# One weighing product per head with the high and low probability columns as the stationary matrix, three probability slots instead of four, new orders

## The chip, the cores and the metric

The kernel runs on one core of a Trainium2 chip. The metric is the device time of one execution in microseconds (us). The time before is 701.28 us, the median of three runs (700.39 to 702.39).

## The reference

A block of three parts works on x of shape (16, 64, 256): 16 batches of 64 query rows.

1. Cross-attention: queries from the normalised x, keys and values from a context of 1601 rows a batch, 16 heads of 16 columns each, softmax over the 1601 keys, an output projection, and the sum with x.
2. Self-attention with rotary positions over the 64 rows of a batch, 16 heads, and again a sum.
3. A routed layer of 8 experts (one for each row, with a capacity of 128 rows an expert), and again a sum.

The change is in the last product of the first part:

```
scores = einsum('bhqd,bhkd->bhqk', q, k) / sqrt(16)
attn   = softmax(scores, axis=-1)
ctx    = einsum('bhqk,bhkd->bhqd', attn, v)
```

All of it is f32 in the reference. The kernel splits f32 numbers into a bf16 high part (the upper half of the f32 word) and a bf16 low part (the rest), and multiplies high by high, high by low and low by high.

## The kernel before, in words

**Batches.** For each of 16 batches, the 1601 context rows are projected to keys and values (letter K in the orders: `project`, lines 812 and 821, in 15 units of work), the keys are stacked by DMA for the products, all scores are taken once for their maxima alone (letter m: `max_scores`, line 844, maxima by DVE at line 1511), and then the batch goes through 13 chunks of 128 keys (the last has 65).

**A chunk.** Two score halves on PE (letter s: `score_half`, line 872), two exponentials on ACT (letter e: `exponentials`, line 1242) into a slot `prob` of 1024 f32 columns (16 heads of 64 queries), one subtraction on POOL (letter p: `low_prob`, line 637; ten of the last batch's on DVE, line 1481) that writes the low parts, packed, into `plow`, and two weighing halves on PE (letter w: `weigh`, line 896). There are `NPAR` = 4 slots of `prob` and `plow`: an exponential into a slot waits until the weighing four chunks back is done.

**Weighing.** The probabilities are the stationary matrix, the values the moving one. A pair of heads (`hp`) makes one product: 128 stationary columns are two heads of 64 queries, and the moving columns are 32 low value columns, 32 high ones and a column of ones for the softmax's sum. With the high columns of the probabilities (every second bf16 of the f32 slot) all 65 columns are multiplied; with the low columns the last 33. Of each result only the blocks in which the head of the queries is the head of the values are used.

**The end of a batch.** DVE takes the reciprocal of the sums (line 1532), multiplies (line 1535, `divided`, letter v), and adds the two value parts in two reductions (line 1548, `attended`, letter a). The next batch's first weighing waits for the multiplication (`out_read`), since the bank `ps_out` is used again.

**Orders.** Each engine works through a string of letters written out in the file (`PE_PROGRAM`, `ACT_PROGRAM`, `DVE_PROGRAM`, `POOL_PROGRAM`); one letter is one call of a function, and its waits are on semaphores. DMAs are issued by SP in a fixed order, some by ACT and POOL at the start.

**Start.** x's first tile is normalised (DVE lines 1399 to 1407, POOL lines 560 and 564), queries are projected, weights are split into high and low parts (`weight_parts`), POOL issues ten DMAs with biases and the second part's weights (lines 585 to 593), and later folds the rotation into biases and weights (`fold`, letter f).

**After the batches.** Self-attention and experts run over eight tiles of 128 rows; this begins while the last batch is still being weighed. A bias is added there by a matmul whose stationary matrix is `pick`, a selecting column repeated 128 times (line 923).

Of the kernel before, what the change touches and what calls it, by code (L numbers as in the profile page):

```python
# [18 lines left out]
P = 128  # L19
D = 256  # L20
KT = D // P
HEADS = 16
DH = D // HEADS
B = 16
SQ = 64
# [9 lines left out]
VW = 66  # L35
OW = 65
NPAR = 4
# [46 lines left out]
def act_frees(b, u):  # L84
# [26 lines left out]
    ("KKKKKKKKKKKKKmmKmmKmKmKmmKmKmKmmKmKmmmKKmmKmKmmKmKmmKKmmKmKmmsKmsmsKmsmsKmwsmswmwsKsmswmwwmKmsswmKwm"  # L111
     "wssmKsmswmwswmsmKsmsmwwsmswmwsmsKmwmsswmKmwwwswswwwswsKmmsswwmKsmswwKmssmKwwmssmwwmKmmsKmmswKmmssKwm"
     "swsmwwmswsKmsmwKmsKmsswmwmKmsswwKmwwwmKwsmKsKmswsmwwsmsKmmssKwmwsmswwmKswmwmwwssKmsmKmwswmmsKmsswwmm"
     "sKsmmswwwsKmKmsswmwmKswmmKmswKswwwmwKswKswwsmmKsmmsKmsmsKwmwwswwmsmKsKwsmKssmKswswmmKmmwwssmKswmmwKm"
     "swwswmswmwwssmKwswmmsKmmwKmKwwmwwswKsKssKsKssmwmKmwsmswwmsmKmwswwmwsmKswmsKmwssmwmKmsmKwsmsmwwwssmKm"
     "wmsswwKmssKmmKmsmwwKmmwwwwKwwsmKsKssKmswsmKmswswmmKmsKsmwwmsKKmmsKswsmmwwswsmwmsKmKmswmKswswmmwsKwms"
     "wwsmwKsmmKsmmsKmmwwwwKwswmwKsswKssmKmssmwKsmwwmssmwKswmmwswsmwKswwsmmKmmKssKmmwwsswwmwmKwmsKsmwwmssK"
     "msmKmmsKmwwmKwmswwKmwsKssKsmsmwKwmssmKswsKwmmswwwmswmKsmsKmsswwwmmswsKmwmKmKmsmKwwsmswwmKswswmmsKmss"
     "wmKmmsKmmwwKwwwsmwKsswKswsmKsmmsKsmwswwwmsmsKmKwmswmwwsmswwKmssmKmwswsmKswmwmKmmswKmsKmmsswwmwsmsKms"
     "mKmmwwwKwwswmwKsswKssmmKmwssmKswmswwmsKsmKswwmmsswwKwsmwsKwwmsmKwmssmKsmmKmwmsKwwsmsmwKwmmssKmKmmKmm"  # L120
     "wwwsKwmswKswsKwswKmmssKwssmwwwsmwswmsmKmswwsmKsmwKsmmKmKwmswmsmKmswmwsmsKwwmwmKmssmKmssmKwwmmwwssKww"
     "wmKswmKssKsmmwswsKmssmwwmwsswmKmssmKwmwwwsswmwKsKsmsmKsmKsmmKmmwwwKmsswmwwwKwsmsmKmssmKmsmKmmwwwKwww"
     "msKssKswwsKmsmsKmwsmKmwsmwsmwwwKsmmsKmwsmswwwmsmKsswmmKmswsmwKmswwmsmsKsmKsmmwKsmsKmKwwwmwwmwKmwswKs"
     "wsmwmsKsmsKssmKmwmwwsmwwsKswmmswsKmwsmswwmKswmsmwsKmmKmsswwmwsKmmswKmwmKsswmKswwswmKmwKmmKswmKssmmws"
     "wwsmsKmsmsKwmmwsswmwwmswKwsmKmsmKmswsmmKmssmwwmwsmwswmsmKmwswsmwmsKmsmwswmsZmwswwsAwswwwwssOswsAwsww"
     "ssOswswwswswsswwswssswwsHsswwsJHswwsTJAVOTSVwwwwwSPPwHwwWJVAP2PTOoWSA2HOoJPPhVTHlWVJS2AToOhSPPhlWPl2"
     "PHAocWOJAV2OHToJhSHhlTlVJcVPTPSWSPP2Wo2PPoxhWlxghcxglx2gcogFhFlFFFFcFFFFFF", 1),
# [94 lines left out]
def build(nc, x, ctxT, wqT, wkT, wvT, bqk, woT, wqkv, wout, brows, wg, weT, be, consts, ones2, out):  # L222
# [3 lines left out]
    with ctx:  # L226
# [22 lines left out]
        vstack = [sb(f"vstack{p}", [P, NCH, HP, VW], bf16) for p in range(2)]  # L249
# [10 lines left out]
        oparts = sb("oparts", [P, 2, 4, 64])  # L260
        orec = sb("orec", [P, 2, 4])
# [21 lines left out]
        wqkv_sb = sb("wqkv_sb", [P, KT, 3 * D])  # L283
# [4 lines left out]
        bias3 = sb("bias3", [SEL, 3 * D])  # L288
        brot3 = sb("brot3", [SEL, 2 * D])
        pick = sb("pick", [SEL, E, P], bf16)  # L290
# [8 lines left out]
        rooms = [flat3(kstack[0]).bitcast(f32), vstack[0][:, :, :, :].rearrange("p c h n -> p (c h n)").bitcast(f32)]  # L299
# [26 lines left out]
        late_rooms = [flat3(kstack[1]).bitcast(f32), vstack[1][:, :, :, :].rearrange("p c h n -> p (c h n)").bitcast(f32)]  # L326
# [19 lines left out]
        late_rooms += [prob[n][:, :] for n in range(3)]  # L346
# [60 lines left out]
        out_inverse, out_read, att_done = sem("out_inverse"), sem("out_read"), sem("att_done")  # L407

# [37 lines left out]
        def v0_stage(u):  # L446

            return prob[(u - KUNITS) // 2][:, (u - KUNITS) % 2 * 512:(u - KUNITS) % 2 * 512 + 512]
# [1407 lines left out]
```

## Time and profile before

| | busy us | share of the span |
|---|---|---|
| PE (matmul) | 671.0 | 96% |
| PE weight loads | 507.2 | 72% |
| DVE | 552.5 | 79% |
| POOL | 549.0 | 78% |
| ACT | 443.4 | 63% |

The profiled execution has a span of 699.7 us from its first instruction to its last; its own time outside the profiler is not listed, and the three timed runs have a median of 701.28 us. The granted clock of PE is full in all 40 slices of the page. A busy time is the union of an engine's instruction durations; a matmul's duration contains its way through the array, which overlaps the next matmul, so the spacing of matmuls has to be read from their start times.

### The profile page before, as it was taken

The numbers are of one execution on the slowest core, as the hardware profiler recorded it, in microseconds if no ns is written. First come the engines' busy times: TensorE is split into PE (matmuls) and PEld (weight loads), VectorE is DVE, ScalarE is ACT, GpSimd is POOL, SyncE is SP. The second block draws the span as 40 slices with busy tenths as digits, with TensorE's granted clock in tenths as the row PEclk, the third lists the DMA queues.
The fourth block names the chain that finished last, engine by engine and source line by source line (L and its number), as shares of the span: only waits on it lengthen the run. The fifth ranks groups of instructions, "written<-read, shape, count | busy, mean of one in ns | idle before, by whom it ended". The sixth has DMA issues, their size and how long they took to land.

```text
span 699.7 us, 21737 instructions
## 1 busy us (share of the span) xinstructions
PE 671.0 (96%) x8632; PEld 507.2 (72%) x8681; DVE 552.5 (79%) x1138; ACT 443.4 (63%) x885; POOL 549.0 (78%) x374
## 2 busy tenths in 40 slices
PE   4799999999999999999999999999999998899897
PEld 2556786877777877787778777877777786677673
DVE  4697877868888878778787868787868788888867
ACT  2446766666666666676767666767675787665830
POOL 7759999999699889798989789889788786723422
PEclk9999999999999999999999999999999999999999
DMA  8587055454445454545353645363543450000212
GB/s 309 143 213 214 27 138 162 99 155 97 150 113 155 105 164 92 160 107 165 93 165 84 178 102 159 85 187 89 169 97 104 100 164 4 2 2 9 91 69 91
DMA packets 45610, 84.20 MB, mean 120 GB/s; under 512 B 8668, under 2 KB 28420, under 8 KB 45508
## 3 DMA queue, kind: packets, MB, share of 16 engines
q1 hardware_dynamic: 43896, 80.13, 41.9%
q0 software_dynamic: 912, 2.14, 1.0%
q8 instruction: 70, 1.15, 0.7%
q10 hardware_dynamic: 704, 0.55, 0.3%
q14 instruction: 28, 0.23, 0.1%
HBM read 36.89 MB, written 6.55 MB: 62 GB/s over the span
## 4 chain that ended last, share of the span: by engine, by line
PE 82%; DVE 5%; DMA 5%; SPq 2%; issue 2%; POOL 2%; ACT 2%; ACTq 0%; DVEq 0%; POOLq 0%
PE ps_kv L821 17%; PE ps_kv L812 16%; PE ps_score L872 12%; PE ps_out L896 12%; PE ps_front L844 12%; PE ps_score L920 2%; SPq L502 2%; DMA kstack<-khigh 2%; PE ps_out L912 1%; DMA cbuf<-in_ctxT 1%; PE ps_kv L783 1%; DMA wq_sb<-in_wqT 1%; PE ps_front L920 1%; PE ps_front L853 1%; PE ps_kv L920 1%
## 5 line engine op out<-in xcount | busy, mean ns | idle before, releaser
L637 POOL TENSOR_TENSOR plow<-prob 128x1024 bf16<-128x1024 f32 (+1 forms) x198 | 372.1, 1898 | 58.8 <-ACT prob L1242 56.3
L1511 DVE TENSOR_REDUCE maxes<-ps_front 128x1 f32<-128x512 f32 (+1 forms) x416 | 267.1, 666 | 57.2 <-PE ps_front L844 53.9
L1242 ACT ACTIVATE prob<-ps_score 128x512 f32<-128x512 f32 (+1 forms) x416 | 236.2, 598 | 71.0 <-PE ps_score L872 61.9
L872 PE MATMUL ps_score<-qstack,kstack 98*128 98x128 bf16 (+1 forms) x1664 | 150.5, 219 | 0.8 <-ACT prob L1242 0.5
L844 PE MATMUL ps_front<-kstack,qstack 96*128 96x512 bf16 (+1 forms) x512 | 145.4, 333 | 2.7 <-DMA kstack<-khigh 1.9
L872 PEld LDWEIGHTS ps_score<-qstack,kstack 98*128 98x128 bf16 (+1 forms) x1664 | 112.1, 98 | 33.7 <-ACT prob L1242 1.9
L896 PE MATMUL ps_out<-vstack,prob 128*128 128x65 bf16 (+1 forms) x1664 | 113.6, 194 | 0.7 <-POOL plow L637 0.3
L821 PE MATMUL ps_kv<-w_hi,cbuf 128*128 128x256 bf16 (+1 forms) x402 | 109.7, 273 | 0.9 <-DVE vstack L1501 0.9
L1494 DVE SCALAR_TENSOR_TENSOR klow<-ps_kv,bcol,khigh 128x512 bf16<-128x512 f32 (+1 forms) x123 | 76.8, 629 | 42.5 <-ACT khigh L1220 42.0
L821 PE MATMUL ps_kv<-w_hi,clow 128*128 128x256 bf16 (+1 forms) x402 | 109.5, 272 | 0.0
L821 PE MATMUL ps_kv<-w_lo,cbuf 128*128 128x256 bf16 (+1 forms) x402 | 109.5, 272 | 0.0
L1220 ACT ACTIVATE khigh<-ps_kv,bcol 128x512 bf16<-128x512 f32 (+1 forms) x123 | 72.7, 593 | 56.0 <-PE ps_kv L812 54.6
L578 POOL TENSOR_TENSOR clow<-cbuf 128x801 bf16<-128x801 f32 (+1 forms) x63 | 96.5, 1542 | 12.8 <-DMA cbuf<-in_ctxT 12.8
L896 PE MATMUL ps_out<-vstack,plow 128*128 128x33 bf16 (+1 forms) x1664 | 102.4, 178 | 0.0
L896 PEld LDWEIGHTS ps_out<-vstack,prob 128*128 128x128 bf16 (+1 forms) x1664 | 91.0, 98 | 15.4 <-POOL plow L637 1.2
L1228 ACT CAST vstack<-ps_kv 128x512 bf16<-128x512 f32 (+1 forms) x105 | 58.2, 554 | 51.7 <-PE ps_kv L821 51.6
L812 PE MATMUL ps_kv<-clow,w_hi 128*128 128x512 bf16 (+1 forms) x245 | 78.0, 331 | 2.4
L812 PE MATMUL ps_kv<-cbuf,w_lo 128*128 128x512 bf16 (+1 forms) x242 | 78.7, 338 | 0.1
L896 PEld LDWEIGHTS ps_out<-vstack,plow 128*128 128x128 bf16 (+1 forms) x1664 | 74.7, 96 | 0.0
L1501 DVE TENSOR_TENSOR vstack<-ps_kv,vstack 128x512 bf16<-128x512 f32 (+1 forms) x105 | 67.7, 645 | 5.5 <-ACT vstack L1228 5.0
L812 PE MATMUL ps_kv<-cbuf,w_hi 128*128 128x512 bf16 (+1 forms) x211 | 66.9, 332 | 0.3 <-DVE klow L1494 0.2
L844 PEld LDWEIGHTS ps_front<-kstack,qstack 96*128 96x128 bf16 x512 | 42.2, 97 | 12.3 <-issue 2.8
(290 smaller groups left out, 858.7 us busy)
## 6 DMA issues: line engine op xcount, KB each, us to landing
kstack<-khigh SPq DMA_DIRECT2D x256, 100.1 KB, 2.2
cbuf<-in_ctxT SPq DMA_DIRECT2D x15, 1601.0 KB, 7.2
kstack<-klow SPq DMA_DIRECT2D x128, 100.1 KB, 2.2
qstack<-q_blocks SPq DMA_DIRECT2D x48, 64.0 KB, 2.3
q_blocks<-qbd SPq DMA_DIRECT2D x16, 128.0 KB, 2.0
cbuf<-in_weT SPq DMA_DIRECT2D x2, 1024.0 KB, 7.8
slot_x<-att_all SPq DMA_DIRECT2D x8, 128.0 KB, 7.1
vstack<-slot_x SPq DMA_DIRECT2D x4, 256.0 KB, 3.6
```

Of the source, the lines that this page charges most:

```text
L578: nc.gpsimd.tensor_tensor(clow[par][:, k, a:a + n], cbuf[par][:, k, a:a + n], c_high(par, k, a, n), ALU.subtract).then_inc(clow_done, 1)
L637: nc.gpsimd.tensor_tensor(plow[slot][0:n, :], prob[slot][0:n, :], p_high(slot, 0, HP * P)[0:n], ALU.subtract).then_inc(plow_gps, 1)
L812: mm = nc.tensor.matmul(ps[:, 0:nn], w[0][:, k, t * P:(t + 1) * P], rhs, start=(j == 0), stop=(j == len(terms) - 1))
L821: mm = nc.tensor.matmul(ps[0:nn, a * D:(a + 1) * D], lhs, w[1][:, k, :], start=(j == 0), stop=(j == len(terms) - 1))
L844: mm = nc.tensor.matmul(ps[:, at:at + nn], qstack[par][0:96, q_at(hp), :], kstack[par][0:96, hp, n0:n0 + nn], start=True, stop=True)
L872: mm = nc.tensor.matmul(ps_score[0:nn, h % NSB, j * P:(j + 1) * P], kstack[par][0:98, hp, n0:n0 + nn], qstack[par][0:98, q_at(hp), :], sta ...
L896: mm = nc.tensor.matmul(o[:, 32 * part:OW], lhs, vstack[par][0:nn, k, hp, 32 * part:OW], start=(k == 0 and part == 0 and hp % 4 == 0), sto ...
L1220: nc.scalar.activation(khigh[:, t, n0:n0 + nn], kv_bank(b, u)[:, 0:nn], ACT.Identity, bias=bcol[:, 1, t:t + 1]).then_inc(high_done, 1)
L1242: nc.scalar.activation(prob[slot][0:nn, e * 512:e * 512 + 512], ps_score[0:nn, h % NSB, :], ACT.Exp)\
L1494: nc.vector.scalar_tensor_tensor(klow[:, t, n0:n0 + nn], kv_bank(b, u)[:, 0:nn], bcol[:, 1, t:t + 1], khigh[:, t, n0:n0 + nn], ALU.add, AL ...
L1501: nc.vector.tensor_tensor(v[:, :, :, 0:32], kv_bank(b, u)[0:rows, 0:nch * D].rearrange("p (c h d) -> p c h d", c=nch, h=HP), v[:, :, :, 32 ...
L1511: nc.vector.reduce_max(maxes[:, hp:hp + len(unit), n], ps[:, 0:len(unit) * nn].rearrange("p (h k) -> p h k", k=nn), AX.X).then_inc(m_free, 1)
```

## The change

The slot of a chunk becomes one f32 array of 16 heads, two parts and 64 columns. The exponential writes part 0 in f32. The subtraction reads part 0 and its upper bf16 halves, and writes the low part as bf16 into the upper halves of part 1. So the 128 upper halves of one head (64 high, 64 low columns) are one stationary matrix with a step of two bf16. The moving matrix is that head's 16 low value columns, 16 high ones and a column of ones: 33 columns. Rows 0 to 63 of the result belong to the high, rows 64 to 127 to the low probabilities; the product of low by low is now included. There are three slots, of 2048 f32 columns each, in the memory of the four slots and their `plow` before.

At the end of a batch ACT copies rows 64 to 127 of the result (letter D, `low_outputs`), DVE adds them to rows 0 to 63, and then takes reciprocal, multiplication and one reduction over 64 rows, where it had 128 rows and two reductions.

To make room, the rotation weights and biases are loaded into parts of `att_all` that are not yet used (`wqk_raw`, `bias_raw`), the load of the former is issued in `fold` 0 instead of at the start, and `pick` is one column, repeated by the operand's access pattern. All four orders are written anew.

```diff
-VW = 66
-OW = 65
-NPAR = 4
+VW = 33
+OW = 33
+NPAR = 3
...
-        prob = [sb(f"prob{p}", [P, HP * P]) for p in range(NPAR)]
-        plow = [sb(f"plow{p}", [P, HP * P], bf16) for p in range(NPAR)]
+        prob = [sb(f"prob{p}", [P, HEADS, 2, SQ]) for p in range(NPAR)]
+        prob_flat = [a[:, :, :, :].rearrange("p h r q -> p (h r q)") for a in prob]
...
+        def p_parts(slot, part):
+            return prob_flat[slot].bitcast(bf16)[:, 1::2].rearrange("p (h r q) -> p h r q", h=HEADS, r=2)[:, :, part, :]
+        def p_columns(slot, h):
+            return prob_flat[slot].bitcast(bf16)[:, 4 * SQ * h + 1:4 * SQ * (h + 1):2]
...
-                nc.gpsimd.tensor_tensor(plow[slot][0:n, :], prob[slot][0:n, :], p_high(slot, 0, HP * P)[0:n],
+                nc.gpsimd.tensor_tensor(p_parts(slot, 1)[0:n], prob[slot][0:n, :, 0, :], p_parts(slot, 0)[0:n],
                                         ALU.subtract).then_inc(plow_gps, 1)
...
-                for part in range(2):
-                    for hp in range(4 * half, 4 * half + 4):
-                        o = ps_out[:, half, (hp % 4) * OW:(hp % 4 + 1) * OW]
-                        lhs = plow[slot][0:nn, hp * P:(hp + 1) * P] if part else p_high(slot, hp * P, P)[0:nn]
-                        mm = nc.tensor.matmul(o[:, 32 * part:OW], lhs, vstack[par][0:nn, k, hp, 32 * part:OW],
...
+                for h in range(HP):
+                    mm = nc.tensor.matmul(ps_out[:, half, h * OW:(h + 1) * OW], p_columns(slot, HP * half + h)[0:nn],
+                                          vstack[par][0:nn, k, HP * half + h, :],
...
+            def low_outputs(b):
+                act.wait_ge(pv_done, NCH * (b + 1))
+                wait(act, out_read, b)
+                wait(act, att_done, b)
+                nc.scalar.copy(oparts[:, :, :, :], ps_out[SQ:2 * SQ, :, 0:HP * OW].rearrange("p a (h c) -> p a h c", c=OW))\
+                    .then_inc(out_low, 1)
...
             def divided(b):
-                dve.wait_ge(pv_done, NCH * (b + 1))
...
+                dve.wait_ge(out_low, b + 1)
+                rows = ps_out[0:SQ, :, 0:HP * OW].rearrange("p a (h c) -> p a h c", c=OW)
+                nc.vector.tensor_tensor(rows, rows, oparts[:, :, :, :], ALU.add).then_inc(out_sums, 1)
+                dve.wait_ge(out_sums, b + 1)
+                nc.vector.reciprocal(orec[:, :, :], rows[:, :, :, 2 * DH]).then_inc(out_inverse, 1)
                 dve.wait_ge(out_inverse, b + 1)
...
+                nc.vector.tensor_tensor(oscaled, rows[:, :, :, 0:2 * DH],
+                                        orec[:, :, :].unsqueeze(3).to_broadcast([SQ, 2, HP, 2 * DH]), ALU.mult)                    .then_inc(out_read, 1)
...
 DVE_PROGRAM = [
-    ("jKKKkKBzKkzKKCKmmmmm...
+    ("jBKkKzKCkKKKKzkKmzmm...
```

## Rows read from the trace of the kernel before

**Rows 1.** The page: the span, then busy time, share and instructions of each engine

```profile
span 699.7 us, 21737 instructions
...
PE 671.0 (96%) x8632; PEld 507.2 (72%) x8681; DVE 552.5 (79%) x1138; ACT 443.4 (63%) x885; POOL 549.0 (78%) x374
```

**Rows 2.** Busy time by stretch: us, busy of each engine, PE clock, DMA

```profile
60.00:580.00 520.00, 516.04 (x7155) 398.20 (x7191) 415.30 (x796) 351.51 (x664) 456.37 (x266) 1.00 0.48 128
580.00:700.00 120.00, 109.33 (x1172) 79.76 (x1178) 95.86 (x254) 66.81 (x177) 48.69 (x59) 1.00 0.12 39
```

**Rows 3.** PE's waits from 60 to 580 us: us in total, times, longest

```profile
PE ps_out L896 <- POOL plow L637: 0.3, 1, 0.3
PE ps_out L896 <- DVE oparts L1535: 0.3, 1, 0.3
```

**Rows 4.** PE's timeline near 304.5 us: start, us, engine, line, operands, count

```profile
304.41 0.39 PE L872 MATMUL ps_score<-qstack,kstack 98*128 98x128 bf16 x4
304.64 0.29 PE L896 MATMUL ps_out<-vstack,prob 128*128 128x65 bf16 x4
304.77 0.25 PE L896 MATMUL ps_out<-vstack,plow 128*128 128x33 bf16 x4
304.87 0.38 PE L872 MATMUL ps_score<-qstack,kstack 98*128 98x128 bf16 x4
```

**Rows 5.** The page's groups of line 896: count, busy us, mean ns, idle before

```profile
L896 PE MATMUL ps_out<-vstack,prob 128*128 128x65 bf16 (+1 forms) x1664 | 113.6, 194 | 0.7 <-POOL plow L637 0.3
...
L896 PE MATMUL ps_out<-vstack,plow 128*128 128x33 bf16 (+1 forms) x1664 | 102.4, 178 | 0.0
L896 PEld LDWEIGHTS ps_out<-vstack,prob 128*128 128x128 bf16 (+1 forms) x1664 | 91.0, 98 | 15.4 <-POOL plow L637 1.2
...
L896 PEld LDWEIGHTS ps_out<-vstack,plow 128*128 128x128 bf16 (+1 forms) x1664 | 74.7, 96 | 0.0
```

**Rows 6.** PE's timeline at the start, six 65-column matmuls, first and last

```profile
16.43 0.19 PE L812 MATMUL ps_kv<-cbuf,w_hi 128*128 128x65 bf16 x1
...
16.59 0.19 PE L812 MATMUL ps_kv<-cbuf,w_lo 128*128 128x65 bf16 x1
```

**Rows 7.** POOL's groups by form: count, busy us, mean ns, idle before

```profile
L637 POOL TENSOR_TENSOR plow<-prob 128x1024 bf16<-128x1024 f32 x183 | 343.8, 1898 | 42.6 <-ACT prob L1242 40.1 <-PE ps_kv L812 0.8 <-PE ps_out L896 0.5
...
L648 POOL TENSOR_TENSOR vstack<-prob,vstack 128x512 bf16<-128x512 f32 x6 | 6.7, 1128 | 3.0 <-ACT vstack L1194 2.9
...
L616 POOL TENSOR_TENSOR brot<-brot 8x512 f32<-8x512 f32 x3 | 3.1, 1032 | 0.2
```

**Rows 8.** DVE's groups by form

```profile
L1548 DVE TENSOR_REDUCE att_all<-oparts 64x128 f32<-64x256 f32 x32 | 13.3, 417 | 0.7
L1535 DVE TENSOR_TENSOR oparts<-ps_out,orec 128x512 f32<-128x512 f32 x16 | 11.1, 692 | 0.6
```

**Rows 9.** ACT's groups by form

```profile
L1242 ACT ACTIVATE prob<-ps_score 128x512 f32<-128x512 f32 x384 | 218.3, 598 | 67.2 <-PE ps_score L872 59.1 <-PE ps_out L896 4.8
...
L1228 ACT CAST vstack<-ps_kv 128x512 bf16<-128x512 f32 x90 | 52.7, 585 | 50.1 <-PE ps_kv L821 50.1
```

**Rows 10.** The timeline from batch 14's last weighing to batch 15's first

```profile
575.74 0.25 PE L896 MATMUL ps_out<-vstack,plow 65*128 65x33 bf16 x4
...
576.79 0.19 DVE L1532 RECIPROCAL orec<-ps_out 128x8 f32<-128x8 f32 x1
577.02 0.69 DVE L1535 TENSOR_TENSOR oparts<-ps_out,orec 128x512 f32<-128x512 f32 x1
...
577.86 0.29 PE L896 MATMUL ps_out<-vstack,prob 128*128 128x65 bf16 x4 [0.26 <-DVE oparts L1535]
```

**Rows 11.** The timeline of the start: POOL's last issue, DVE's variance, POOL's root, PE

```profile
18.26 0.81 POOL L593 DMA_DIRECT2D wg_sb<-in_wg  x1
...
19.77 0.15 DVE L1407 TENSOR_SCALAR ve<-mv 128x1 f32<-128x1 f32 x1
...
20.01 0.58 POOL L560 TENSOR_TENSOR rs<-ve,half_neg 128x1 f32<-128x1 f32 x1 [0.94 <-DVE ve L1407]
...
21.98 0.33 PE L773 MATMUL ps_kv<-cst,h 128*128 128x128 f32 x1 [2.06 <-POOL h L564]
```

More of the change, by code:

```diff
@@ L248, in build @@
         kstack = [sb(f"kstack{p}", [P, HP, SKP], bf16) for p in range(2)]
-        vstack = [sb(f"vstack{p}", [P, NCH, HP, VW], bf16) for p in range(2)]
+        vflat = [sb(f"vstack{p}", [P, NCH * HEADS * VW], bf16) for p in range(2)]
+        vstack = [a[:, :].rearrange("p (c h n) -> p c h n", c=NCH, h=HEADS) for a in vflat]
         qstack = [sb(f"qstack{p}", [P, HP, P], bf16) for p in range(2)]
-        prob = [sb(f"prob{p}", [P, HP * P]) for p in range(NPAR)]
-        plow = [sb(f"plow{p}", [P, HP * P], bf16) for p in range(NPAR)]
+        prob = [sb(f"prob{p}", [P, HEADS, 2, SQ]) for p in range(NPAR)]
+        prob_flat = [a[:, :, :, :].rearrange("p h r q -> p (h r q)") for a in prob]
         maxes = sb("maxes", [P, HP, NPIECE])
@@ L287, in build @@
         wg_sb = sb("wg_sb", [P, KT, E])
[L288 removed]
+        bias3 = sb("bias3", [SEL, D])
         brot3 = sb("brot3", [SEL, 2 * D])
[L290 removed]
+        pick = sb("pick", [SEL, E], bf16)
         picked = sb("picked", [SEL, 2, E])
@@ L345, in build @@
         pT = [a.rearrange("p (h n) -> p h n", h=HP) for a in kbd_flat]
-        late_rooms += [prob[n][:, :] for n in range(3)]
+        late_rooms += [prob_flat[n][:, 0:HP * P] for n in range(3)]
         late_used += [0, 0, 0]
@@ L922, in product3 @@
                 for i, (cols, row, bias) in enumerate(biases):
-                    mm = nc.tensor.matmul(dst[:, cols], pick[:, row, :], high(bias), start=False,
+                    mm = nc.tensor.matmul(dst[:, cols], pick[:, row:row + 1].to_broadcast([SEL, P]), high(bias), start=False,
                                           stop=(i == len(biases) - 1), skip_group_check=True)
@@ L1081, in experts @@
                          lambda k: we_low[k][:, cols],
-                         [(slice(a * D, (a + 1) * D), 2 * pair + a, bias3[:, 2 * D:3 * D]) for a in range(2)])\
+                         [(slice(a * D, (a + 1) * D), 2 * pair + a, bias3[:, :]) for a in range(2)])\
                     .then_inc(ev["e_ps"], 1)
@@ L1347, in _ @@
                     copy_shift(*next(shifts))
+                if letter == "D":
+                    low_outputs(next(outputs))
                 if letter == "Z":
@@ L1543, in attended @@
                     dve.wait_ge(zeros_sent, 16 * (E + BY_SLOT))
[L1544 to L1548 removed]
+                dst = att_all[SQ * (b % 2):SQ * (b % 2) + SQ, b // 2 * D:b // 2 * D + D]
+                nc.vector.reduce_sum(dst.rearrange("p (h d) -> p h d", h=HEADS),
+                                     oscaled.rearrange("p a h (r d) -> p (a h) d r", r=2), AX.X).then_inc(att_done, 1)
             def constants():
```

175 lines of the change are left out of this document (85 added, 90 removed).

## The prediction

> **What bounds the kernel now.** I read four things in turn. First the busy shares: TensorE (PE) is busy 96% of a span of 699.7 us, no other engine over 79% [rows 1]. Busy time of pipelined matmuls can overstate, so second the stretches: between 60 and 580 us, where the batches run, PE is busy 516.0 of 520 us and GpSimd (POOL) 456.4 [rows 2]. Third PE's waits in that stretch: the two that touch this change come to 0.3 us each, once in 520 us [rows 3]. So PE's instruction stream is the clock of that stretch, and whatever shortens the stream shortens the kernel, until another engine runs out: POOL has 64 us to spare there (520 - 456). The last 120 us differ: PE is busy 109.3 of 120 [rows 2]; there, chains across engines decide.
>
> Fourth the spacing of the weighing matmuls, since the mean durations contain the pipeline's drain. A weighing half is four 65-column matmuls with the high columns, then four 33-column ones with the low columns. The first four take 0.13 us from start to start of the next group (32.5 ns each), the second four 0.10 us (25 ns each) [rows 4]. There are 1664 of either kind [rows 5], in 416 such pairs of groups.
>
> The profile's span is 699.7 us against a median of 701.28: 1.6 us lie around the span. I sum against the span and add 1.6.
>
> **The weighing.** A half becomes eight matmuls, one per head, each with 128 stationary and 33 moving columns. The number of matmuls and weight loads stays 3328. The 1664 wide ones become narrow: 1664 x (32.5 - 25) ns = 12.5 us less on PE, if a narrow matmul keeps its 25 ns. Halving the columns doesn't halve the time: 33 columns cost 25 ns, not half of 32.5.
>
> What is new is that every stationary operand is now read with a step of two bf16; before, the low half was packed. Its load might be the limit at 33 columns. Bounds: at most 32.5 ns, since the high group keeps that with stepped loads [rows 4]; its 32.5 come from the 65 columns, for 65-column matmuls whose stationary is packed also start 0.16 us / 5 = 32 ns apart [rows 6]. At least 25 ns, the shortest that the trace shows for 33 columns. A stepped load lasts 98 ns, a packed one 96 [rows 5]: next to no difference. I take 25 ns. Ends of the range: -12.5 us at 25; at 32.5 the high half gains nothing and the low half loses as much, +12.5 us.
>
> The Trainium skill speaks against the term: "TensorE: Matmul & The Clock Gate", section "Back-to-back issue gap", gives about 81 ns per matmul for a sustained stream of load and matmul pairs at 128 columns. If loads set such a floor, fewer columns would save nothing and the weighing would give 0. The trace disagrees: four 128-column score matmuls, each with its own load, take 0.23 us, 57 ns each [rows 4], so the measurement decides.
>
> **The subtraction for the low part** (POOL, ten on VectorE, DVE) now writes every second bf16 in runs of 64 instead of a packed row. No row shows that. POOL's packed form takes 1898 ns; a 512-element POOL operation with f32 output (elements 4 bytes apart) takes 1032 ns, one with operands broken into runs of 32 takes 1128 [rows 7], 9% more. So bounds 1.89 to 2.07 us; I take 1.90, since the step in bytes is that of an f32 row. Cover: POOL's 64 us. At 2.07 its load in the stretch rises by some 185 x 0.17 = 31 us to 488, of about 508 left. It hides, though thinly: in the first windows POOL is fuller than on average. The exponentials' writes in runs of 64 and V's in runs of 16: V's cast, already in runs of 32, takes 585 ns for 512 elements against 598 for the unbroken exponential [rows 9]; 0, bounds +-5%, hidden by both engines' idle time.
>
> **The end of a batch.** Before: reciprocal, then multiplication, 0.20 + 0.69 us on DVE [rows 10]. After: ACT copies the low 64 rows (528 elements; about 0.60, by the exponential [rows 9]), DVE adds (528/512 x 0.69 = 0.71 [rows 8]), reciprocal, multiplication. That is 1.3 us more work and two more hand-offs, estimated at 0.2 each from the 0.15 between the multiplication's end and the next weighing [rows 10]: 1.7 us more, some 3.0 us from a batch's last weighing to the next one's first. The reductions fall from two of 0.417 [rows 8] to one of 512 elements, about 0.7. DVE gains 0.6 us a batch, ACT 0.6, both off the bound. Queued behind the wait on DVE are maxima (which free the front banks) and K's low parts; behind ACT's copy, exponentials.
>
> What covers it is PE's other work between these weighings. Counting letters of the new PE order with the spacings of the trace, that is 3.3 to 7.4 us at 13 of the 15 boundaries, 1.1 us at the first and 0.2 at the last. The first loses 3.0 - 1.1 = 1.9 us. The last lacks 2.8, but is followed by a batch that ACT, DVE and POOL pace anyway, and DVE is already waited for there [rows 10]; I take +1.5 of 0 to 2.8. If the cover fails everywhere (other work ahead in the two queues), it is up to 15 x 1.7 = 26 us.
>
> **Three slots for four.** Between a chunk's last scores and its first weighing lies the exponential (0.6), the subtraction (1.9) and hand-offs (0.4): 2.9 us. In the new order PE has a median of 4.8 us of other work there (5.8 before); in batches 0 to 13 just two chunks have less, by 1.9 us together, and they stand at the first boundary, already counted. So 0 here; bounds 0 to +6, since exponentials must now wait for a weighing three chunks back instead of four.
>
> **Startup.** PE waits 2.06 us for the second query tile's normalised rows, whose chain starts with DVE's variance at 19.77; POOL starts the root at 20.01 after issuing DMAs until 19.07 [rows 11]. The new DVE order takes that variance after two low parts instead of four, so POOL starts right after its issues: 1.0 us less. The weights' split moves ahead into DVE's idle time. The rotation weights' load goes from POOL's queue at the start to the bias fold; its reader is several steps later. Bounds -2 to +1. The 38 bias matmuls with a broadcast column: 0.
>
> **Sum:** -12.5 - 1.0 + 1.9 + 1.5 = -10.1; 699.7 - 10.1 + 1.6 = 691.2. Forecast **691 us**.
>
> **Rivals.**
> *Longer path and fewer slots eat the gain.* Both lengthen PE's dependence on three other engines; the order was written out for assumed durations, and PE waits where one is late. For it: the median cover fell from 5.8 to 4.8 us, and the path grew at every boundary. Against: PE waited 0.3 us on this path in 14 batches. With 0.6 us lost per boundary and some 2 us to slots, 9 + 2 = 11 us: 702.
>
> *Stepped loads set the pace* (the other side). At 33 columns the load no longer hides behind the matmul, on all 3328. It decides from about 28 ns: from there the gain, 1664 x (32.5 - x) - 1664 x (x - 25), falls under the 2.4 us of the other terms. At 32.5: 691 + 25 = 716; at 30, 691 + 17 = 708. Against: 98 to 96 ns.
>
> *POOL becomes the bound.* It decides where 456 + 185 x d exceeds 516, d = 0.32 us, a subtraction of 2.2 us. At 2.4: 456 + 93 = 549, 33 us over the old stretch, 735; against it, the largest growth in a like row is 9%. At 2.07 only the full early windows suffer, some 4 us: 695.
>
> *It saves nothing*, for 25 ns may hold only in groups of four: 699 to 704.
>
> **How the numbers follow.** Forecast 0.66 (685 to 698), path and slots 0.15 (698 to 705), stepped loads 0.08, POOL 0.08, nothing saved 0.03. What this kernel's measurement tells from no change is about 0.3%, 2.1 us. Faster by more: all of the forecast, 0.05 of path and slots, 0.04 of the small ends of loads and POOL: 0.75. Same: 0.07 of path and slots, 0.03 of the others: 0.10. Slower: 0.15. Range 685 to 704; above it lies most of the loads and POOL cases (0.13), below it 0.06 for a startup and tail better than counted.
>
> **What would show it.** In the profile after: eight 33-column matmuls in 0.20 us (0.26 for the stepped-load case); POOL's subtraction at 1.9 us (over 2.2 is the POOL case), with POOL's waits for exponentials shrinking from the idle time it has; PE busy at 99% in the batches, its waits on the attention rows once at the first boundary and once at the last (at most boundaries: the path case); the wait for the second query tile at about 1 us. A loss of PE time in the last 120 us of over 4 us would also make the prediction wrong: there the orders differ most, and I counted only one boundary.

## The result, and the profile after

The changed kernel takes 724.24 us (median of six runs, 722.85 to 729.34), the kernel before beside it 701.92 (700.39 to 702.57): 1.0331 times as long, with an interval of 1.0302 to 1.0361. I forecast 691 us and a range that ended at 704: sign and size are wrong.

The page of the changed kernel first: PE is busy 12 us longer, in a span 27 us longer [rows 1].

```profile
span 726.6 us, 21820 instructions
...
PE 683.2 (94%) x8681; PEld 506.5 (70%) x8681; DVE 561.5 (77%) x1138; ACT 458.6 (63%) x901; POOL 550.1 (76%) x376
```

What the sum spoke of came about, as far as single instructions go. PE's timeline: eight weighing matmuls of 33 columns take 0.20 us (302.71 to 302.91), 25 ns each, as taken from [rows 4].

```profile
302.71 0.36 PE L906 MATMUL ps_out<-vstack,prob 128*128 128x33 bf16 x8
302.91 0.38 PE L885 MATMUL ps_score<-qstack,kstack 98*128 98x128 bf16 x4
```

The groups of the page say the same of the two operations that no row of before showed: the subtraction takes 1898 ns and the stepped load 97 ns [rows 5, 7].

```profile
L650 POOL TENSOR_TENSOR prob<-prob 128x1024 bf16<-128x1024 f32 (+1 forms) x198 | 372.3, 1898 | 65.6 <-ACT prob L1252 63.8
...
L906 PEld LDWEIGHTS ps_out<-vstack,prob 128*128 128x128 bf16 (+1 forms) x3328 | 121.7, 97 | 22.6 <-issue 2.2
```

The stretches show where the time went (columns as in [rows 2]). From 60 to 580 us PE is busy 513.2 of 520. The last 147 us end 27 us later than before; PE is idle 23 of them, where it was idle 11 of 120, and its mean granted clock is 0.93, in one stretch 0.83. Before, it was 1.00 throughout.

```profile
60.00:580.00 520.00, 513.20 (x7117) 389.03 (x7116) 416.65 (x792) 362.10 (x671) 456.97 (x266) 0.99 0.48 128
...
580.00:727.00 147.00, 123.91 (x1263) 89.08 (x1260) 103.78 (x259) 72.13 (x187) 48.67 (x60) 0.93 0.10 32
...
660.00:680.00 20.00, 14.96 (x162) 10.92 (x163) 13.42 (x34) 12.09 (x34) 7.39 (x8) 0.83 0.08 28
```

PE's waits from 580 us on have two long ones that the kernel before lacks. The longest of the kernel before there is 1.3 us, on DVE's `klow`.

```profile
PE ps_out L916 <- DVE prob L1604: 4.0, 2, 3.8
PE ps_out L1071 <- DVE mask L1676: 3.0, 1, 3.0
```

I divide each kernel at the start of its last group of weighing matmuls, and call the time from there to the start of PE's last group of matmuls the tail (self-attention and experts). These are the two groups in the kernel before, and then in the one after: the tail grew from 91 to 113 us.

```profile
604.87 0.25 PE L896 MATMUL ps_out<-vstack,plow 65*128 65x33 bf16 x4
...
696.17 0.39 PE L923 MATMUL ps_front<-bias,pick 72*128 72x256 bf16 x2
```

```profile
610.29 0.37 PE L906 MATMUL ps_out<-vstack,prob 65*128 65x33 bf16 x8
...
723.06 0.39 PE L933 MATMUL ps_front<-bias,pick 72*128 72x256 bf16 x2
```

### The profile page after: what moved, and what is told of

It is laid out like the page before. It is cut to its first block, busy times and chain, and to the rows that moved or that the text cites. A ratio compares the mean times of both kernels' runs of the same rounds, so it can differ in the third digit from the quotient of the medians.

```text
span 726.6 us, 21820 instructions
## 1 busy us (share of the span) xinstructions
PE 683.2 (94%) x8681; PEld 506.5 (70%) x8681; DVE 561.5 (77%) x1138; ACT 458.6 (63%) x901; POOL 550.1 (76%) x376
## 4 chain that ended last, share of the span: by engine, by line
PE 81%; DMA 5%; DVE 3%; SPq 3%; issue 3%; ACT 3%; POOL 2%; ACTq 0%; POOLq 0%; DVEq 0%
PE ps_kv L834 17%; PE ps_kv L825 14%; PE ps_score L885 12%; PE ps_front L857 12%; PE ps_out L906 10%; DMA kstack<-khigh 3%; SPq L512 2%; PE ps_score L930 2%; PE ps_front L930 2%; PE ps_kv L930 2%; PE ps_out L922 2%; POOL prob L650 1%; PE ps_kv L796 1%; SPq L505 1%; DMA wq_sb<-in_wqT 1%
## 5 line engine op out<-in xcount | busy, mean ns | idle before, releaser
L650 POOL TENSOR_TENSOR prob<-prob 128x1024 bf16<-128x1024 f32 (+1 forms) x198 | 372.3, 1898 | 65.6 <-ACT prob L1252 63.8
L1252 ACT ACTIVATE prob<-ps_score 128x512 f32<-128x512 f32 (+1 forms) x416 | 236.2, 597 | 70.6 <-PE ps_score L885 43.4
L885 PE MATMUL ps_score<-qstack,kstack 98*128 98x128 bf16 (+1 forms) x1664 | 155.8, 221 | 2.2 <-ACT prob L1252 2.0
L857 PE MATMUL ps_front<-kstack,qstack 96*128 96x512 bf16 (+1 forms) x512 | 147.5, 336 | 7.4 <-DMA kstack<-khigh 6.5
L906 PEld LDWEIGHTS ps_out<-vstack,prob 128*128 128x128 bf16 (+1 forms) x3328 | 121.7, 97 | 22.6 <-issue 2.2
L885 PEld LDWEIGHTS ps_score<-qstack,kstack 98*128 98x128 bf16 (+1 forms) x1664 | 113.4, 99 | 32.8 <-ACT prob L1252 4.4
L906 PE MATMUL ps_out<-vstack,prob 128*128 128x33 bf16 (+1 forms) x3328 | 132.9, 178 | 2.6 <-DVE prob L1501 1.4
L1238 ACT CAST vstack<-ps_kv 128x512 bf16<-128x512 f32 (+1 forms) x105 | 60.8, 580 | 49.8 <-PE ps_kv L834 49.4
L825 PE MATMUL ps_kv<-cbuf,w_hi 128*128 128x512 bf16 (+1 forms) x246 | 80.6, 341 | 1.3 <-DVE klow L1514 1.2
L825 PE MATMUL ps_kv<-cbuf,w_lo 128*128 128x512 bf16 (+1 forms) x246 | 80.8, 341 | 0.0
L834 PEld LDWEIGHTS ps_kv<-w_lo,cbuf 128*128 128x128 bf16 (+1 forms) x402 | 39.9, 99 | 8.1 <-issue 0.5
L834 PEld LDWEIGHTS ps_kv<-w_hi,cbuf 128*128 128x128 bf16 (+1 forms) x402 | 39.8, 99 | 6.0 <-issue 1.0
```

Source lines behind the costliest of these rows:

```text
L650: nc.gpsimd.tensor_tensor(p_parts(slot, 1)[0:n], prob[slot][0:n, :, 0, :], p_parts(slot, 0)[0:n], ALU.subtract).then_inc(plow_gps, 1)
L825: mm = nc.tensor.matmul(ps[:, 0:nn], w[0][:, k, t * P:(t + 1) * P], rhs, start=(j == 0), stop=(j == len(terms) - 1))
L834: mm = nc.tensor.matmul(ps[0:nn, a * D:(a + 1) * D], lhs, w[1][:, k, :], start=(j == 0), stop=(j == len(terms) - 1))
L857: mm = nc.tensor.matmul(ps[:, at:at + nn], qstack[par][0:96, q_at(hp), :], kstack[par][0:96, hp, n0:n0 + nn], start=True, stop=True)
L885: mm = nc.tensor.matmul(ps_score[0:nn, h % NSB, j * P:(j + 1) * P], kstack[par][0:98, hp, n0:n0 + nn], qstack[par][0:98, q_at(hp), :], sta ...
L906: mm = nc.tensor.matmul(ps_out[:, half, h * OW:(h + 1) * OW], p_columns(slot, HP * half + h)[0:nn], vstack[par][0:nn, k, HP * half + h, :] ...
```

## The experiments

Each experiment gives its edit and what follows; the times stand in one table behind them. "Old" orders are those of the kernel before. Differences are against runs of the kernel before on the same chip.

**The narrow product alone (e1).** Old kernel and orders; all 3328 weighing matmuls have 33 columns. Left out: the high columns with the low value columns.

```diff
-mm = nc.tensor.matmul(o[:, 32 * part:OW], lhs, vstack[par][0:nn, k, hp, 32 * part:OW],
+cols = slice(32 - 32 * part, OW - 32 * part)
+mm = nc.tensor.matmul(o[:, cols], lhs, vstack[par][0:nn, k, hp, cols],
```

> The kernel before with one edit: the matmul on the high part moves 33 columns in place of 65, as the matmul on the low part does (the high part's product with the low values is left out). Each weighing then has the changed kernel's price, 8 matmuls of 25 ns, and orders, four slots and the out path stay as before. Theory T (the loss sits in the new orders): 689 to 694 us at a granted clock of 1.0. Rival N (a narrow moving side leaves TensorE too little work and its clock falls): 710 to 725 us with the clock below 0.99. Rival P (TensorE's saved time was not on the path): 699 to 703 us. Rival S (three slots and the longer out path): as T, since neither is in this kernel.

Measured: -8.2 us. Narrow columns help, by two thirds of the 12.5 that I counted. The tail is as before.

**The old product with the new orders (e2), and with the new tail alone (e3).** e2 takes all new order strings, e3 the new ones only from the letter Z on (the last batches' end and the tail; four letters w that the new tail lacks stand ahead of Z).

```diff
 # e3, PE_PROGRAM, around Z
-...ZmwswwsAwswwwwssOswsAwsw...
+...wwwwZmwswsAswswAswswswwssOws...
```

> The kernel before with the changed kernel's four written orders (ScalarE's without its 16 new letters D); old product, four slots. Theory T: 718 to 736 us and a granted clock below 0.99, since the orders alone bring the waits. Rivals N and S: 699 to 704 us at a clock of 1.0, since the product, the slots and the out path are the old ones.

> The kernel before with its own orders up to the letter Z (the last batch) and the changed kernel's orders from there on. Theory T, if the tail's order holds most of the loss: 715 to 725 us, with the 90 us behind the last weighing grown by 15 to 21 us. If T holds but the loss sits in the batches' order: 699 to 704 us. Rivals N and S: 699 to 704 us.

Measured: +27.2 and +20.4. The new orders slow down a kernel that has none of the new product, and most of it is the tail's order. e3's waits are those of the kernel after, to the digit:

```profile
PE ps_out L906 <- DVE prob L1585: 4.0, 2, 3.8
...
PE ps_out L1061 <- DVE mask L1657: 3.0, 1, 3.0
```

**Narrow product and new orders (e4), and that with three slots (e8).** e4 is e1 with the new orders; e8 lets it use three of its four slots.

```diff
 # e8
+SLOTS_USED = 3
-slot = i % NPAR
+slot = i % SLOTS_USED
...
-wait(act, pv_done, i - NPAR + 1)
+wait(act, pv_done, i - SLOTS_USED + 1)
```

> Both edits: the kernel before with 33 columns in every weighing matmul and with the changed kernel's orders (without D); four slots and the old out path stay. Theory T: 712 to 726 us, near the changed kernel's 724, with the clock below 0.99. Rival N: 710 to 726 us also. Rival S (slots and out path): 686 to 696 us, since both are the old ones. Read with the run of narrow matmuls alone and the run of the orders alone it tells whether the two add up.

> The old product with 33 columns and the new orders (721.5 us), with three of its four probability slots used. If the third slot's loss is what still parts it from the changed kernel (724.2 us): 723 to 726 us, with more exponentials waiting for a slot and keys' waits of 5 us or more. If the longer out path is: 720 to 722.5 us.

Measured: +19.9 and +18.2. Product and orders add up (27.2 - 8.2 = 19.0). The third slot costs nothing that can be seen: the two intervals overlap.

**The tail's two waits.** In e5 two of e3's POOL letters I (the conversion of expert weights) change place, one to a later and one to an earlier point; in e6 PE multiplies idle matrices (56 and 44 matmuls of 128 columns) during e3's two long waits.

```diff
 # e5, POOL_PROGRAM, its end
-...RrssRtItstssRYRIRYgYgggg
+...RrssRttstIIssRYRRYgYgggg
 # e6
+if t == 4: pe.wait_ge(ev["x2"], t + 1); keep_busy(0, 56)
+if g == 2: pe.wait_ge(ev["lg"], b); keep_busy(1, 44)
```

> The old product with the new tail (722 us), with two letters of GpSimd's order moved: the third and fourth conversion of expert weights (1.88 us each) run behind the scatter's reads, away from the two VectorE instructions that took 2.66 us (usually 0.41) and 1.76 us (usually 0.16) beside them. If those collisions make TensorE's two long waits of the tail (3.78 and 3.01 us): the waits shrink by some 1.9 and 1.6 us, less clock is lost behind them, 714 to 719 us. Rival (the waits come from TensorE's order, which leaves no other work there): the waits move to what is late next, 720 to 723 us.

> The old product with the new tail (722 us), with idle matmuls (56 and 44 of 128 columns, results unused) put on TensorE into its two long waits of the tail, so that it works while it waits. If the low clock behind these waits costs real time: the stretches at half clock behind them vanish, and with them the 4 us of TensorE time lost in them, 716 to 720 us. If the tail is bound by the chain between the engines and not by TensorE's speed: 721 to 724 us, the clock at 1.0 all the same.

Measured: +14.1 and +14.3, against e3's +20.4; the tail shrinks by some 4 us in either. e6's interval lies clear of e3's; e5's runs spread from 715.1 to 723.1 us and its interval overlaps e3's, so for e5 the reading rests on the trace: the shorter tail, and two waits that are halved.

```profile
PE ps_out L906 <- DVE prob L1585: 2.1, 2, 1.9
...
PE ps_out L1061 <- DVE mask L1657: 1.4, 1, 1.4
```

In e6 the clock stays full where e3's falls; the stretches of e3, then of e6:

```profile
650.00:670.00 20.00, 14.81 (x138) 9.48 (x131) 13.13 (x36) 10.21 (x30) 9.16 (x10) 0.83 0.06 20
675.00:695.00 20.00, 15.57 (x136) 12.56 (x135) 11.24 (x37) 7.57 (x20) 4.79 (x6) 0.91 0.20 64
```

```profile
650.00:670.00 20.00, 17.93 (x213) 13.37 (x212) 14.83 (x41) 11.97 (x36) 9.48 (x11) 1.00 0.06 21
675.00:695.00 20.00, 18.43 (x192) 14.89 (x193) 11.91 (x41) 7.08 (x20) 4.79 (x6) 1.00 0.22 77
```

So both causes work in the tail, the waits and the clock behind them. In either run some 16 of the tail's 20 us remain, but not all of that is of another origin: e6 takes away the clock's part and leaves the two waits in place, and e5 leaves about half of them.

**The changed kernel with the old tail (e7), with four slots (g3), with both (g4).** e7's old tail has some letters behind Z shifted, as three slots want it; g3 is the change with `NPAR = 4`; g4 is g3 with the old tail, without four letters w that the new batch orders have ahead of Z.

```diff
 # g3, g4
-NPAR = 3
+NPAR = 4
```

> The changed kernel with the tail's orders of the kernel before (from the letter Z on, six letters shifted so that three slots suffice); product, slots, out path and the batches' orders are the changed kernel's. Theory T (the tail's order holds most of the loss): 702 to 709 us, that is 724 less 15 to 22. Rivals: if the new product itself needs the longer tail, 718 to 726 us.

> The changed kernel with four slots in place of three, nothing else. If the third slot costs: 715 to 721 us. If it costs nothing, as in the old product under these orders: 722 to 726 us.

> The changed kernel with four slots and the tail's orders of the kernel before from the letter Z on (no letters shifted in TensorE's order; ScalarE's two letters D added). Theory T: the changed kernel's last weighing (610.7 us) and the old tail behind it (91 us), 702 to 707 us, so 17 to 22 us off the changed kernel. If the old tail does not fit the new batches: 710 us or more.

Measured: +9.3, +22.6 and +1.2. Four slots change nothing by themselves (724.56 us, the change 724.24). g3 and g4 differ in the tail's order alone, and by 21 us. The stretch from the last weighing to the end of PE's work, g3 and then g4:

```profile
607.27:719.21 111.94, 97.35 (x861) 68.43 (x860) 78.47 (x225) 50.18 (x137) 35.46 (x43) 0.94 0.12 37
```

```profile
607.06:698.61 91.55, 88.29 (x847) 63.09 (x847) 72.56 (x219) 48.43 (x134) 30.28 (x37) 1.00 0.15 49
```

Both begin it at 607 us. Of the 20.4 us between them PE is idle 11.3 more (14.6 against 3.3) and busy 9.1 more; at a clock of 0.94 some 13 us run at half speed, which can account for up to 6.7 of the 9.1, and 14 more matmuls stand behind the last weighing (861 against 847). Of the idle 11.3 some 6.4 are waits for the two results of the long waits (7.0 against 0.6). In e7 the shifted scores waited for exponentials in the last batch, the mean clock from 580 to 618.5 us was 0.74, and its weighing ended only at 618.4: its short tail was paid for ahead of it, and neither time that was expected came.

**The new product with the old orders (f1, g2), and searched orders (f2).** f1: four slots, old orders, only the letter D added (POOL's order keeps the changed kernel's beginning). g2 moves 7 letters D and 6 letters v of f1 by one or two places. f2 is f1 with some hundred letters of the four orders moved, by a search for shorter waits.

```diff
 # f1
-NPAR = 3
+NPAR = 4
 # ACT_PROGRAM: one D per batch, ahead of DVE's v
```

> The changed kernel with four slots (8 KB of on-chip memory more per partition, which is there) and with the four orders of the kernel before; only ScalarE's 16 letters D are added (GpSimd's order keeps the changed kernel's beginning). So product and out path are new, orders and slot count old. Theory T: the run of narrow matmuls under old orders (693) plus what the longer out path costs, 694 to 700 us, clock at 1.0, faster than both kernels. Rival (new product or out path cost what the changed kernel lost): 712 us or more.

> The new product with old orders and four slots (712 us), with 7 of ScalarE's 16 letters D and 6 of VectorE's 16 letters v moved by one or two places, earlier where the copy started over 0.8 us behind the last weighing, later where ScalarE stood idle for it. If the place of these letters holds the out path's loss: 703 to 709 us. If what is queued behind them decides: 710 to 714 us.

> As the run above, with some hundred letters of the four orders moved by up to six places, to shorten waits at the batch boundaries and in the tail. Theory T (order is what decides): 684 to 696 us, below the run with the old orders. If the old orders are already as good as such moves can make them: 694 to 702 us.

Measured: +10.3, +10.1 and +13.5. Under the old orders the new product loses although its matmuls are cheaper, and a shift of D and v by one or two places changes nothing. f2 came out slower than either of its two expectations.

**The old product with the new batch orders (f3).** The strings of e2 (no letter D) up to Z, the old ones from there.

```diff
 # all four PROGRAMs: new letters up to Z, old letters from Z on
```

> The kernel before with the changed kernel's orders for the batches and its own from the letter Z on; old product, four slots, old out path. The last weighing of the narrow run came 6 us later with the new orders than with the old: if that is the batches' order alone, 705 to 710 us. If the batches' order costs nothing by itself: 700 to 703 us.

Measured: +6.1. With g4's +1.2 this shows that the batch orders suit the new product (712.0 us under the old ones, 703.2 under the new) and not the old one.

**The long out path alone (f4), and with the narrow product (g1).** In the kernel before, ACT copies half of the sums at each boundary and DVE adds them; nothing else changes.

```diff
+nc.scalar.copy(oparts[0:64], ps_out[64:128, :, 0:4 * OW]...)    # ACT, letter D
...
+nc.vector.tensor_tensor(oparts[0:64], rows[0:64, :, :, 0:64], oparts[0:64], ALU.add)
 nc.vector.reciprocal(...)
```

> The kernel before with the changed kernel's longer out path alone: ScalarE copies half of the output sums (letter D, 0.6 us) and VectorE adds them (0.7 us) before the reciprocal; these two results are overwritten and not used. 16 boundaries. By the prediction's terms it costs 1.9 us at the first boundary and 1.5 at the last: 703 to 706 us. If other boundaries are uncovered too: 706 to 712 us. If all is covered: 701 to 703 us.

> The kernel before with both edits: 33 columns in every weighing matmul, and the longer out path (ScalarE's copy, VectorE's add, results not used); old orders, four slots, old product. If the two add up (less 8.2, plus 10.4): 702 to 706 us, and the 8 us that the new product took beyond that are its own layout. If a faster TensorE only meets the out path's waits sooner: 708 to 713 us, and the new product's layout is free.

Measured: +10.4 and +2.6 (-8.2 + 10.4 = 2.2: they add up). Two small operations at each of 16 batch ends cost 10.4 us, about 0.65 each. f4's timeline of one boundary shows the chain:

```profile
305.99 0.25 PE L897 MATMUL ps_out<-vstack,plow 65*128 65x33 bf16 x4
...
306.28 0.58 ACT L1257 COPY oparts<-ps_out 64x512 f32<-64x512 f32 x1 [0.76 <-PE ps_out L897]
...
307.11 0.67 DVE L1542 TENSOR_TENSOR oparts<-ps_out,oparts 64x512 f32<-64x512 f32 x1
...
308.06 0.69 DVE L1547 TENSOR_TENSOR oparts<-ps_out,orec 128x512 f32<-128x512 f32 x1
...
308.90 0.29 PE L897 MATMUL ps_out<-vstack,prob 128*128 128x65 bf16 x4 [0.23 <-DVE oparts L1547]
```

PE's own wait for the out path is short here (0.23). What costs is behind it in the queues; f4's waits from 60 to 610 us:

```profile
PE ps_front L845 <- DVE maxes L1521: 2.3, 7, 0.5
PE ps_score L873 <- ACT qstack L1249: 1.4, 1, 1.4
PE ps_score L873 <- ACT prob L1243: 1.3, 4, 0.5
```

The kernel before has no wait for maxima in this stretch, e1 one of 0.2. While DVE waits for the copy, the maxima that free the front banks stand behind it. All of PE's waits from 60 us to the last weighing sum up to 10.0 us here, to 4.2 in the kernel before; the other 4 or 5 us stand in no listed wait. So the queue behind the wait is shown for a part of the 10.4, and for the rest it is argued.

**The bank freed earlier (h1, h2).** The sum goes to SBUF, and the next batch may weigh after the addition; the multiplication reads SBUF. h1 is g4 with this and three letters m later, h2 is f1 with this.

```diff
-nc.vector.tensor_tensor(rows, rows, oparts, ALU.add).then_inc(out_sums, 1)
+nc.vector.tensor_tensor(oparts, rows, oparts, ALU.add).then_inc(out_read, 1)
```

> The changed kernel with four slots and the old tail (703.2 us), with two edits: the out path's add writes its sum to on-chip memory, so that the output banks are free after it and not after the multiplication; and three letters m of batches 2 and 4 stand one to three places later, where TensorE had waited 1.5 and 1.1 us for keys. If the held banks and those waits cost: 697 to 701 us, faster than both kernels. If the chain on VectorE decides, which is as long as before: 701 to 705 us.

> The new product with the old orders and four slots (712 us), with the add writing to on-chip memory and the output banks free after it. If the hold on the banks makes the new product's rest: 703 to 708 us. If it is something else (its layout, what waits behind VectorE): 710 to 713 us.

Measured: +16.7 and +31.3, 15 and 21 us more than g4 and f1, and none of the expected times. The multiplication is the reason. DVE's groups of h2, and then of f1, where its first input lies in PSUM:

```profile
L1556 DVE TENSOR_TENSOR oparts<-oparts,orec 64x512 f32<-64x512 f32 x16 | 33.1, 2071 | 0.5
```

```profile
L1557 DVE TENSOR_TENSOR oparts<-ps_out,orec 64x512 f32<-64x512 f32 x16 | 10.9, 682 | 0.5
```

The 16 multiplications last 22.2 us longer, and the kernel 21. PE pays at the maxima that stand behind them: its wait for them from 60 us to the last weighing is 1.5 us in f1, and 19.6 in h2:

```profile
PE ps_front L857 <- DVE maxes L1531: 19.6, 14, 7.3
```

So these two couldn't tell what an earlier release is worth, but they show what an operation on DVE costs that holds up the maxima.

| kernel | median us | ratio to before, interval | last weighing starts | tail |
|---|---|---|---|---|
| before | 701.9 | | 605 | 91.3 |
| after | 724.2 | 1.0331, 1.0302 to 1.0361 | 610 | 112.8 |
| e1 narrow product | 693.4 | 0.9888, 0.9858 to 0.9919 | 595 | 91.5 |
| e2 new orders | 728.8 | 1.0389, 1.0360 to 1.0418 | 610 | 112.5 |
| e3 new tail | 722.0 | 1.0293, 1.0266 to 1.0320 | 603 | 111.4 |
| e4 narrow, new orders | 721.5 | 1.0291, 1.0260 to 1.0322 | 601 | 113.4 |
| e8 e4, three slots | 721.5 | 1.0270, 1.0240 to 1.0299 | 604 | 111.9 |
| e5 e3, conversions moved | 717.5 | 1.0236, 1.0185 to 1.0288 | 603 | 107.0 |
| e6 e3, waits filled | 717.7 | 1.0207, 1.0176 to 1.0239 | 606 | 107.5 |
| e7 after, old tail shifted | 712.6 | 1.0138, 1.0109 to 1.0167 | 618 | 91.2 |
| g3 after, four slots | 724.6 | 1.0318, 1.0286 to 1.0350 | 607 | 111.9 |
| g4 g3, old tail | 703.2 | 1.0019, 0.9996 to 1.0041 | 607 | 91.7 |
| f1 new product, old orders | 712.0 | 1.0143, 1.0102 to 1.0183 | 614 | 91.2 |
| g2 f1, letters shifted | 712.1 | 1.0151, 1.0126 to 1.0175 | 615 | 91.3 |
| f2 f1, searched orders | 715.2 | 1.0184, 1.0146 to 1.0221 | 617 | 91.4 |
| f3 new batch orders | 707.9 | 1.0074, 1.0053 to 1.0096 | 612 | 91.3 |
| f4 long out path | 712.1 | 1.0144, 1.0105 to 1.0182 | 614 | 91.4 |
| g1 e1 and f4 | 704.6 | 1.0035, 1.0021 to 1.0049 | 608 | 91.4 |
| h1 g4, early release | 718.5 | 1.0234, 1.0213 to 1.0255 | 621 | 91.6 |
| h2 f1, early release | 733.1 | 1.0437, 1.0419 to 1.0456 | 638 | 92.1 |

## Why the prediction was wrong

The parts, each measured in a kernel that has it: narrow product -8.2 (e1), tail order +20.4 (e3), batch orders +6.1 (f3), and what the change has beyond e8, the out path and the layout, +4.1 (22.3 - 18.2). They sum up to 22.4 us; the change costs 22.3. Each has an interval of some +-2 us, and the last part is itself a difference from the change, so the test lies in the first three: 18.3 together, where the kernel that has all three took +18.2 with three slots (e8) and +19.9 with four (e4).

**The step that failed: the last 120 us.** The prediction had said that "there the orders differ most, and I counted only one boundary": the sum held +1.5 us for the last boundary and nothing for the order behind it. That order costs 20 to 21 us, in the old product (e3) and in the new (g3 against g4). The tail is 91 to 92 us with the old order and 107 to 113 with the new one, whatever the product, the slots and the out path are. I had read from [rows 2] that chains across engines decide there, and then walked none of them. The profile after shows one of them link by link, around 660 us:

```profile
660.36 0.71 POOL L694 TENSOR_TENSOR kstack<-kstack,khigh 128x256 f32<-128x256 f32 x1
660.42 2.67 DVE L1604 TENSOR_SCALAR prob<-kstack,mv,rs 128x256 f32<-128x256 f32 x1 [1.14 <-POOL rs L700]
661.04 1.88 POOL L732 TENSOR_TENSOR clow<-cbuf 128x1024 bf16<-128x1024 f32 x1
...
663.14 0.69 PE L916 MATMUL ps_out<-cst,prob 128*128 128x128 f32 x2 [3.78 <-DVE prob L1604]
```

DVE's normalisation lasts 2.67 us and ends with the expert conversion on POOL (L732); 3 us earlier the same operation took 0.40. PE waits 3.78 us. The new order put conversions beside such operations; e5 moved two of them, and the waits halved. PE's clock in these stretches (us, PE busy, clock, DMA):

```profile
655.00:659.00 4.00, 4.00 (x33) 1.00 0.00 0
659.00:663.10 4.10, 0.37 (x3) 0.86 0.18 64
663.10:666.50 3.40, 3.35 (x16) 0.50 0.11 39
666.50:669.90 3.40, 3.40 (x17) 0.67 0.00 0
```

Behind the wait the granted clock is 0.50, the level of 1.2 GHz, while PE is busy. Half speed over 3.4 us and 0.67 over 3.4 more is 1.7 + 1.1 = 2.8 us of PE's speed lost, on top of the 3.78 waited. e6 shows that it is the idle time that brings it: with idle matmuls in the wait the clock stays 1.00. So of the 20.4 us between g4 and g3 some 6.4 are these two waits and up to 6.7 the clock. The other waits of the tail, some 5 us more in all, and the rest weren't taken apart, nor which of the four strings brings them.

**The weighing** (-12.5): mechanism right, 25 ns a matmul; -8.2 came. From 60 us to the last weighing and counted from start to start, the 1664 narrowed matmuls take 43.4 us in e1's trace where they took 54.1: 26.1 ns each, so 10.7 us of the 12.5. PE's listed waits from 60 us to the last weighing rise by 1.0 us (4.2 to 5.2, e1); the other 1.5 us I can't place.

**The end of a batch** (+3.4 in all, 26 "if the cover fails everywhere"): the term was mis-sized, under the old orders by three times (f4: 10.4). I took PE's letters between the two weighings as cover, and they cover the weighing; they don't cover what stands behind DVE's wait, which I had named and priced at nothing. In the new batch orders the path fits better: with the layout it costs +4.1 there (above), near the 3.4 of the sum. The last boundary of the kernel after shows the path (3.0 us expected from weighing to weighing, 2.9 measured, and the only wait of this kind, 0.54).

```profile
580.57 0.36 PE L906 MATMUL ps_out<-vstack,prob 65*128 65x33 bf16 x8
...
580.97 0.60 ACT L1268 COPY oparts<-ps_out 64x528 f32<-64x528 f32 x1 [0.69 <-PE ps_out L906]
...
581.60 0.71 DVE L1552 TENSOR_TENSOR ps_out<-ps_out,oparts 64x528 f32<-64x528 f32 x1
...
582.62 0.68 DVE L1557 TENSOR_TENSOR oparts<-ps_out,orec 64x512 f32<-64x512 f32 x1
...
583.45 0.33 PE L906 MATMUL ps_out<-vstack,prob 128*128 128x33 bf16 x6 [0.54 <-DVE oparts L1557]
```

So product, out path and batch orders together come to +1.2 us (g4): the 10 us forecast up to there weren't gained either.

**Right:** the subtraction at 1.90 us and hidden; three slots at 0 (g3, e8); the startup, where PE's wait for the second query tile is 1.27 us for 2.06, 0.8 less of the 1.0 counted [rows 11] (no run shows whether the end of the kernel came earlier by it).

**The rivals.** Of "longer path and fewer slots" the first half is true for the old orders and the second isn't. Stepped loads and POOL are out by their rows in the kernel after (25 ns a matmul, 1898 ns a subtraction). None named the tail.

**Open.** f1 (712.0) is 7 us slower than g1 (704.6), which has its orders (but for POOL's beginning), its out path and its number of matmuls. The traces show two differences. Up to the last weighing PE waits 3.8 us for POOL's subtraction in f1, 0.6 in g1. And the granted clock is 0.50, the level of 1.2 GHz, in three stretches of f1, the first of them right behind two such waits (0.82 and 1.28 us, until 89.67); in g1 it is 1.00 up to the last weighing.

```profile
89.80:93.20 3.40, 3.40 (x35) 0.50 0.71 163
229.80:233.20 3.40, 3.40 (x12) 0.50 0.52 121
601.80:605.20 3.40, 3.40 (x15) 0.50 0.01 2
```

That is up to 5.1 us of PE's speed, and it isn't this run alone: the mean clock is 0.992 to 0.995 in f1's four runs, 0.995 to 1.000 in g1's ten. Whether the layout or POOL's beginning makes POOL late there wasn't separated. No kernel with the full product beat the one before; g4 equals it.

## What to carry to other kernels

A new order of instructions is a change of its own, and where engines take turns it can outweigh what it was written for: walk its chains link by link in each stretch where PE isn't full, or run it alone with the old arithmetic. When an operation with a wait goes into an in-order queue, price what stands behind it, not only the path that it lies on. And a long PE wait can cost again at a lower clock afterwards (here 2.8 us behind a wait of 3.78).

## What the runs showed of the hardware

**DVE beside POOL.** Here DVE operations whose inputs all lie in SBUF lasted, at worst, until POOL paused. In h2 the worst multiplication, 0.68 us long in f1, took 7.91; the timeline shows POOL beside it, without a gap from 127.26 to 137.66 us:

```profile
127.26 5.59 POOL L650 TENSOR_TENSOR prob<-prob 128x1024 bf16<-128x1024 f32 x3
...
130.29 7.91 DVE L1556 TENSOR_TENSOR oparts<-oparts,orec 64x512 f32<-64x512 f32 x1
...
132.82 1.52 POOL L589 TENSOR_TENSOR clow<-cbuf 128x800 bf16<-128x800 f32 x1
...
134.29 1.89 POOL L650 TENSOR_TENSOR prob<-prob 128x1024 bf16<-128x1024 f32 x1
...
136.14 1.52 POOL L589 TENSOR_TENSOR clow<-cbuf 128x800 bf16<-128x800 f32 x1
```

It ends at 138.20, 0.5 us after POOL's first pause (136.14 + 1.52 = 137.66). The inputs' place alone isn't slow: at 239.4 and 610.1 us no POOL instruction runs beside the multiplication, and it takes 0.68 us. The Trainium skill, "SBUF — State Buffer", section "Who interferes with whom", has a rule for it: a DVE instruction with two SBUF inputs contends with a GpSimd instruction that reads SBUF, the ports that the two share are an exclusive lock, and the order of issue decides which of them blocks. The trace agrees (2071 against 682 ns on average), and shows that the wait can outlast several POOL instructions. The second wait of the tail is of this kind too: an operation of 8 columns lasts 1.76 us, until the conversion beside it ends, and PE waits 3.02.

```profile
686.60 1.89 POOL L732 TENSOR_TENSOR clow<-cbuf 128x1024 bf16<-128x1024 f32 x1
...
686.75 1.76 DVE L1672 TENSOR_TENSOR prob<-prob,cst 128x8 f32<-128x8 f32 x1
...
689.06 0.17 PE L1071 MATMUL ps_out<-mask,tri_bf 128*128 128x8 bf16 x1 [3.02 <-DVE mask L1676]
```
